# A mixture-of-experts layer: the combine stage replaced by weighing at PSUM and an adding indirect DMA

## What is computed

```python
gate_scores = softmax(x @ Wg + bg)                     # x: the layer-normed (2, 1024, 256)
topk_scores, topk_idx = top_k(gate_scores, 2)
topk_scores = topk_scores / (sum(topk_scores) + 1e-08)
for e in range(8):
    h = gelu(x @ W1[e] + b1[e])                        # W1[e]: 256x1024
    y = h @ W2[e] + b2[e]                              # W2[e]: 1024x256
    output = output + y * combine_w[..., e:e + 1]      # combine_w: topk_scores at the chosen experts
return x + output
```

## Time and profile before

| what | value |
|---|---|
| median of 3 runs | 1556.93 us (1554.15 to 1557.86) |
| profiled execution, span from first to last instruction | 1558.3 us |
| TensorE busy | 1257.4 us (81%) |
| TensorE weight loads | 752.1 us (48%) |
| VectorE busy | 840.2 us (54%) |
| ScalarE busy | 759.1 us (49%) |
| GpSimd busy | 279.8 us (18%) |
| mean granted TensorE clock | 0.886 |

### The profile page before, as it was taken

One profiled execution on the slowest core, in us unless ns is written; L12 is line 12 of the kernel. 1 busy time (PEld: TensorE's weight loads), 2 busy tenths in 40 slices (PEclk: granted clock), 3 DMA queues, 4 the chain that ended last, 5 costly groups with the idle time before them and its releaser, 6 DMA issues. The chain is left out here.

```text
span 1558.3 us, 26085 instructions
## 1 busy us (share of the span) xinstructions
PE 1257.4 (81%) x8850; PEld 752.1 (48%) x8851; DVE 840.2 (54%) x1883; ACT 759.1 (49%) x1473; POOL 279.8 (18%) x491
## 2 busy tenths in 40 slices
PE   4849999999999757974446999789875299999992
PEld 2313444444444245433125553554363299999991
DVE  4868777777777035336899545653255122322323
ACT  2815777777777713553654668235520033333330
POOL 1831222222222201102000000211023401111110
PEclk8958999999999967997558999989985599999996
DMA  5670312331230042000001000060026201111115
GB/s 198 210 225 15 70 36 69 74 72 33 73 70 16 13 122 90 1 1 21 1 0 32 1 2 1 27 230 1 5 61 196 86 28 37 37 34 37 37 33 170
DMA packets 63104, 96.09 MB, mean 62 GB/s; under 512 B 11057, under 2 KB 51923, under 8 KB 61459
## 3 DMA queue, kind: packets, MB, share of 16 engines
q1 hardware_dynamic: 56214, 78.14, 17.1%
q0 software_dynamic: 4672, 14.50, 2.8%
q10 hardware_dynamic: 2112, 2.10, 0.4%
HBM read 65.15 MB, written 29.17 MB: 61 GB/s over the span
## 5 line engine op out<-in xcount | busy, mean ns | idle before, releaser
L816 DVE CUSTOM_DVE_ANT_0 faded_scores_sb<-banks,inner_sb 128x1024 f32<-128x1024 f32 x256 | 304.5, 1223 | 102.2 <-PE banks L647 101.1
L915 ACT ACTIVATE xt_sb<-banks 128x512 f32<-128x512 f32 x344 | 179.0, 604 | 73.4 <-PE banks L654 73.4
L654 PE MATMUL banks<-q_stack_sb,k_stack_sb 99*128 99x128 bf16 (+3 forms) x960 | 181.0, 297 | 5.8 <-ACT xt_sb L915 2.6
L647 PE MATMUL banks<-k_stack_sb,q_stack_sb 96*128 96x512 bf16 (+3 forms) x704 | 163.9, 339 | 13.7 <-POOL ident_b_sb L744 9.4
L654 PEld LDWEIGHTS banks<-q_stack_sb,k_stack_sb 99*128 99x128 bf16 x960 | 71.7, 97 | 158.9 <-ACT xt_sb L915 66.6
L2074 PEld LDWEIGHTS banks<-slots_xt_sb,tile_w_sb 128*128 128x128 f32 x1248 | 146.6, 193 | 3.3 <-issue 1.4
L2074 PE MATMUL banks<-slots_xt_sb,tile_w_sb 128*128 128x128 f32 x1248 | 146.9, 276 | 1.0 <-DVE tile_b_sb L2172 1.0
L2086 PE MATMUL banks<-experts_w_sb,xt_sb 128*128 x624 | 141.2, 379 | 1.3 <-issue 1.3
L2086 PEld LDWEIGHTS banks<-experts_w_sb,xt_sb 128*128 128x128 f32 x624 | 115.5, 190 | 15.8 <-issue 1.7
L2120 ACT ACTIVATE slots_xt_sb<-banks 128x256 f32<-128x256 f32 x39 | 14.9, 383 | 213.9 <-PE banks L2060 213.9
L915 ACT ACTIVATE probs_sb<-banks 128x512 f32<-128x512 f32 x168 | 87.3, 605 | 34.2 <-PE banks L654 34.2
(11 more groups left out here) (303 smaller groups left out, 2081.8 us busy)
## 6 DMA issues: line engine op xcount, KB each, us to landing
experts_w_sb<-in_L_ffn_W SPq DMA_DIRECT2D x16, 1024.0 KB, 11.8
k_stack_sb<-k_parts SPq DMA_DIRECT2D x48, 256.0 KB, 4.9
q_stack_sb<-q_parts SPq DMA_DIRECT2D x96, 128.0 KB, 3.4
q_parts<-parts_sb SPq DMA_DIRECT2D x16, 384.0 KB, 2.7
k_parts<-parts_sb SPq DMA_DIRECT2D x16, 384.0 KB, 3.4
slots_x<-zeros_sb POOLq DMA_DIRECT2D x1, 5031.0 KB, 21.8
slots_x_sb<-slots_x SPq DMA_DIRECT2D x39, 129.0 KB, 2.0
xt_sb<-outputs_y SPq DMA_DIRECT2D x8, 512.0 KB, 6.5
```

The source lines that it names most:

```text
L647: last = pe.matmul(k.ps[:, 2 * (tile % 2) + half, lo - half * G:hi - half * G], stacks.q[0:ROWS, g % 3, version, h, j * P:(j + 1) * P], st ...
L654: return pe.matmul(k.ps[:, bank, at:at + hi - lo], stacks.k[0:ROWS + PARTS, g // 2 % 2, version, h, kt * P:(kt + 1) * P], stacks.q[0:ROWS ...
L816: dve.tensor_tensor_reduce(out=junk[:, tile % 2, :], in0=tile_scores(tile), in1=inner[:, window(tile)], scale=1.0, scalar=-3.0e38, op0=ALU ...
L915: act.activation(out, k.ps[:, bank_of((exp_done, u + 1)), :], ACT.Exp).then_inc(exp_done, 1)
```

## The change

A slot row gets three more values: both choices' experts (plus one) and both weights, next to the token's number, now stored minus `LATER` = 4096 so that an empty slot (zero) can be told apart. The weights are computed earlier in `route`, ahead of the scatters, and GpSimd waits for them. In `experts`, `take_rows` compares both choices with the tile's expert, multiplies by the weights, and adds the two to a share per row; the output row is the token, or one of 128 spare rows for an empty slot. The copy of y from PSUM multiplies by the share. The output has 128 spare rows; at the head of the block SyncE's queue writes `k.x` (x plus weighted b2) to it and zeros to the spare rows. Each scatter adds to the output in HBM, and waits on GpSimd for the scatter before it. The combine block and `outputs_y` are gone; the host slices the spare rows off.

```diff
-SLOT = D + 2
+SLOT = D + 5
+LATER = 2 * T
...
@@ route, GpSimd and VectorE @@
-            pool.wait_ge(numbered, 2)
+            pool.wait_ge(numbered, 4)
...
-            dve.tensor_scalar(xn[:, :, D + 1], at[:, :, 0], 1.0, None, ALU.add).then_inc(numbered, 1)
+            dve.tensor_scalar(xn[:, :, D + 1:D + 3], at[:, :, 0:2], 1.0, None, ALU.add).then_inc(numbered, 1)
...
+            step(dve.tensor_tensor(ssum[:, :], best[:, :, 0], best[:, :, 1], ALU.add))
+            step(dve.tensor_scalar(ssum[:, :], ssum[:, :], 1e-8, None, ALU.add))
+            step(dve.reciprocal(inv[:, :], ssum[:, :]))
+            for n in range(2):
+                dve.tensor_tensor(xn[:, :, D + 3 + n], best[:, :, n], inv[:, :], ALU.mult).then_inc(numbered, 1)
             dve.wait_ge(counted, 1)
...
-            step(dve.tensor_tensor(ssum[:, :], best[:, :, 0], best[:, :, 1], ALU.add))
-            step(dve.tensor_scalar(ssum[:, :], ssum[:, :], 1e-8, None, ALU.add))
-            step(dve.reciprocal(inv[:, :], ssum[:, :]))
+            dve.wait_ge(numbered, 4)
             for n in range(2):
-                step(dve.tensor_tensor(r.weight[:, n, :], best[:, :, n], inv[:, :], ALU.mult))
-                step(dve.tensor_tensor(hot[:, n, :, :], hot[:, n, :, :], wide(r.weight[:, n, :]), ALU.mult))
+                step(dve.tensor_tensor(hot[:, n, :, :], hot[:, n, :, :], wide(xn[:, :, D + 3 + n]), ALU.mult))
...
@@ experts, SyncE @@
-            sp.dma_start(idle[:, :], k.idle_in).then_inc(idle_in, 16)
+            sp.dma_start(spare[:, :], k.idle_in).then_inc(idle_in, 16)
+            sp.dma_start(out[0:T, :].rearrange("(t p) n -> p t n", p=P), k.x[:, :, :]).then_inc(out_in, 16)
+            sp.dma_start(out[T:T + P, :], k.zeros[:, 0:D]).then_inc(out_in, 16)
             bodies(sp, step)
...
@@ experts, GpSimd @@
                 pool.wait_ge(y_copied, n + 1)
+
+                if s > 0:
+                    pool.wait_ge(y_out[s - 1], (i + 1) * 16)
+                elif not (isinstance(i, int) and i == 0):
+                    pool.wait_ge(y_out[BODY - 1], i * 16)
                 pool.nop(nofuse=True)
-                pool.indirect_dma_start(out=scratch.y[:, :], out_offset=bass.IndirectOffsetOnAxis(ap=to[:, s:s + 1], axis=0),
-                                        in_=ys[:, s, :], in_offset=None).then_inc(y_out[s], 16)
+                pool.indirect_dma_start(out=out[:, :], out_offset=bass.IndirectOffsetOnAxis(ap=to[:, s:s + 1], axis=0),
+                                        in_=ys[:, s, :], in_offset=None, compute_op=ALU.add).then_inc(y_out[s], 16)
+            pool.wait_ge(out_in, 2 * 16)
             bodies(pool, step)
...
@@ experts, VectorE: take_rows, copy of y @@
-                dve.tensor_tensor(is_best[:, u:u + 1], xs[:, u, D + 1:SLOT], r.owned[:, tile], ALU.is_equal).then_inc(row_step, 1)
-                dve.wait_ge(row_step, 2 * (i * BODY + s) + 1)
-                dve.scalar_tensor_tensor(out=is_best[:, u:u + 1], in0=is_best[:, u:u + 1], scalar=float(T), in1=xs[:, u, D:D + 1],
-                                         op0=ALU.mult, op1=ALU.add).then_inc(row_step, 1)
-                dve.wait_ge(row_step, 2 * (i * BODY + s) + 2)
-                dve.tensor_tensor(to[:, u:u + 1], is_best[:, u:u + 1], idle[:, tile], ALU.max).then_inc(to_taken, 1)
+                dve.tensor_tensor(shares[:, u, :], xs[:, u, D + 1:D + 3], r.owned[:, tile].to_broadcast([P, 2]),
+                                  ALU.is_equal).then_inc(row_step, 1)
+                dve.wait_ge(row_step, 3 * (i * BODY + s) + 1)
+                dve.tensor_tensor(shares[:, u, :], shares[:, u, :], xs[:, u, D + 3:SLOT], ALU.mult).then_inc(row_step, 1)
+                dve.scalar_tensor_tensor(out=to[:, u:u + 1], in0=xs[:, u, D:D + 1], scalar=float(LATER), in1=spare[:, :],
+                                         op0=ALU.add, op1=ALU.min).then_inc(to_taken, 1)
+                dve.wait_ge(row_step, 3 * (i * BODY + s) + 2)
+                dve.tensor_tensor(share[:, u:u + 1], shares[:, u, 0:1], shares[:, u, 1:2], ALU.add).then_inc(row_step, 1)
...
-                dve.tensor_copy(ys[:, s, :], k.ps[:, 6, s * D:(s + 1) * D]).then_inc(y_copied, 1)
+                dve.wait_ge(row_step, 3 * n + 3)
+                dve.tensor_scalar(ys[:, s, :], k.ps[:, 6, s * D:(s + 1) * D], share[:, s:s + 1], None, ALU.mult).then_inc(y_copied, 1)
...
@@ program: combine (42 lines) and its call taken out @@
-            experts(k, r, scratch)
-            combine(k, r, scratch, out)
+            experts(k, r, scratch, out)
```

More of the change, by code:

```diff
@@ L1999, in _, with experts @@
                 dve.tensor_tensor(k.x[:, t, :], k.x[:, t, :], k.ps[:, 5 + t % 2, 0:D], ALU.add).then_inc(b2_added, 1)
-def experts(k, r, scratch):
+def experts(k, r, scratch, out):
     nc = k.nc
     k.next_block()
+    out_in = k.sem("out_in")
     x_in = [k.sem(f"x_in{u}") for u in range(2)]
@@ L2018, in experts @@
         xs = k.sb(c, "slots_x", [P, 2, SLOT])
-        is_best = k.sb(c, "is_best", [P, 2])
+        shares = k.sb(c, "shares", [P, 2, 2])
+        share = k.sb(c, "share", [P, 2])
         to = k.sb(c, "output_row", [P, 2], U32)
-        idle = k.sb(c, "idle_rows", [P, SLOT_TILES])
+        spare = k.sb(c, "spare_rows", [P, 1])
         xst = k.sb(c, "slots_xt", [P, 2, KD, P])
@@ L2190, in _ @@
                 dve.wait_ge(y_out[s], (NB + (s == 0)) * 16)
[L2193 to L2233, removed]
 INS = ["x", "L0_attn_W_down_kv", "L0_attn_W_up_k", "L0_attn_W_up_v", "L0_attn_Wq", "L0_attn_Wo",
@@ L2333, in program @@
             r.slot = k.sb(c, "slot", [P, 2, NT], U32)
-            r.weight = k.sb(c, "choice_weight", [P, 2, NT])
             r.owned = k.sb(c, "tile_owned", [P, SLOT_TILES])
@@ L2338, in program @@
             scratch.x = k.slots_x
-            scratch.y = nc.dram_tensor("outputs_y", (2 * T + SLOT_TILES * P, D), F32).ap()
             r.b1 = k.sb(c, "experts_b1", [P, E, FT])
@@ L2381, in layout @@
     a["c_iota"] = np.repeat(np.arange(IOTA, dtype=np.float32)[None, :], P, axis=0)
-    a["c_idle"] = np.ascontiguousarray(np.arange(SLOT_TILES * P, dtype=np.float32).reshape(SLOT_TILES, P).T)
-    a["c_numbers"] = np.ascontiguousarray((SLOT_TILES * P + np.arange(T, dtype=np.float32)).reshape(NT, P).T)
+    a["c_idle"] = T + np.arange(P, dtype=np.float32)[:, None]
+    a["c_numbers"] = np.ascontiguousarray((np.arange(T, dtype=np.float32) - LATER).reshape(NT, P).T)
     a["c_before"] = np.triu(np.ones((P, P), np.float32), 1)
@@ L2406 @@
          for n, a in arrays.items()}
-    out = nc.dram_tensor("out_0", (B, S, D), F32, kind="ExternalOutput").ap()
+    out = nc.dram_tensor("out_0", (T + P, D), F32, kind="ExternalOutput").ap()
     program(nc, d, out)
     got = run_bass_kernel_spmd(nc, [{f"in_{n}": a for n, a in arrays.items()}], core_ids=[0])
-    return got.results[0]["out_0"]
+    return np.asarray(got.results[0]["out_0"])[0:T].reshape(B, S, D)
```

## The result

The changed kernel takes 1567.31 us (median of 4 runs, 1566.79 to 1568.56) beside 1557.39 us for the kernel before: a ratio of 1.0069, 95% interval 1.0055 to 1.0083. It is about 10 us slower, where 6 us faster was forecast; it lies in the predicted range, and on the side of rival 1. The profiled execution's span is 1565.0 us.

A forecast was written before the change was run, and what follows sets the result against it. TensorE was taken to bound the experts' loop, the scatter's landing only just behind. End −24.7, preset +6.5 and loop +12.4 summed to −5.8 us: span 1552.5, or 1551 us on the median, range 1541 to 1582.

The forecast's parts named there:

- rival 1: Experts' loop, first row operation's wait: the adding scatter's landing becomes the bound; slower, up to 1589 us; chance 0.32.
- The accumulate, A: Each scatter in the experts' loop: adding to HBM costs 0.80 us extra, bounds 0 and 2.0.
- turning point of 1.1: Extra us per adding scatter at which the whole edit was forecast to gain 0.
- third list of descriptors: Part of the adding scatter's extra cost: 0.15 us taken, at most 0.28 for a list of 128.
- The read's later answer: Part of the adding scatter's extra cost: reading HBM answers later than SBUF, +0.15 us.
- The law of the loop: Experts' loop: time per tile is max(7.245, 7.09 + x/2, 6.41 + x), x being the added copy-to-choice time.
- middle branch: Time per tile 7.09 + x/2: from x = 0.31 to 1.36, half of each added us is lost.
- The small operations: Experts' loop: a fourth row operation 0.10 and two waits of 0.05 each; together 0.20 us, bounds 0.05 and 0.45.
- The preset: Start of the experts' stage: output stores ahead of the first slot fetch delay it by 6.5 us, bounds 0 and 9.7.
- The end: After the last scatter's issue: 3.6 us instead of 28.3, with 0.4 of closing, so −24.7 us.
- The gate weights: Moved ahead of the wait for the counts, where VectorE idles 1.30 us: about 0.97 us covered, nothing added.
- the clock: TensorE's clock stays at 1.00, the 2.4 GHz level, through the loop's gaps; no loss charged.

The follow-up runs named there:

- e1_plain: The changed kernel with the add taken out of its scatters, so each overwrites its output rows; 1540.64 us, ratio to the kernel before 0.9893.
- e7_rows64: The changed kernel with scatters of only the first 64 of 128 rows, at full width; single run 1553.48 us.
- e6_half: The changed kernel with scatters adding only the first 128 of 256 values of a row, to a tensor of its own; single run 1561.75 us.
- e9_before_add: The kernel before with scatters that add, to outputs_y filled with zeros by one more DMA; 1601.76 us, ratio 1.0286.
- e2_order: The changed kernel with the choice of weights ahead of the row operations in VectorE's order; 1541.47 us, ratio to the kernel before 0.9901.
- e3_preset: The changed kernel with the output preset moved into the routing stage as five stores; 1559.9 us, ratio to the kernel before 1.0006.
- e5_before_order: The kernel before with the choice of weights ahead of the row operations, nothing else; ratio 1.0006 over 12 runs.

## Why the prediction was wrong

The sign was wrong because of one term, the accumulate's, which was put at little more than half of what it took; the mechanism and its place were right.

**The accumulate, A.** The step that failed is "Second, the accumulate itself", A = 0.80. Measured: 3.8 us instead of 2.4, A = 1.4, above the turning point of 1.1. From copy to row operations it is 5.37 us in the mean, past the 4.9 that the prediction named as the sign of rival 1. DMA view of one plain scatter of the kernel before, from its issue to the row operations (40 slices of 0.065 us, busy share of the DMA engines), then of one adding scatter (slices of 0.099 us):

```profile
DMA  0000000000000000000000089798600000000000
...
DMA packets 48, 0.13 MB, mean 50 GB/s; under 512 B 16, under 2 KB 16, under 8 KB 48
```

```profile
DMA  0000000000000000000009951559999652000000
...
DMA packets 144, 0.13 MB, mean 33 GB/s; under 512 B 16, under 2 KB 144, under 8 KB 144
```

The plain one's packets run from 1.50 to 1.89 us after the issue, the adding one's from 2.07 to 3.36. So the start of the packets is 0.57 us later, where I took 0.15 for a third list of descriptors and thought 0.28 the most, from a zero fill that has no index per row; the issue on GpSimd grew by 0.59, which covers it. Little of that goes by the row: half the rows took 0.135 us off. What the rest is stays open. The packets last 1.29 us instead of 0.39, +0.90, where I took 0.50: there are 144, one per row, instead of 48 of up to 4 KB. The read's later answer, +0.15, doesn't show: the stretch after the last packet is 0.57 us, 0.69 before. The rule that an adding DMA moves at half the copy's rate, which the page gives for ring collectives (the Trainium skill, Collectives: The Full Stack, section "The bandwidth ceiling: the fold count and why AG ≠ RS ≠ AR") doesn't carry over: by it q0 would hold an engine 2 × 0.37 = 0.74 us a scatter, by an estimate; it held one 14.3% × 320 us / 38 = 1.20 us a scatter (its 5472 packets are those of 38 scatters), three times the plain 0.37:

```profile
q0 software_dynamic: 5472, 4.98, 14.3%
```

**The law of the loop** held. x is the mean of copy to row operations between 1300 and 1500 us, less 3.74 for the kernel before, and the period over 36 tiles:

| kernel | x, us | law | measured |
|---|---|---|---|
| e1_plain | 0.24 | 7.245 | 7.248 |
| e7_rows64 | 0.95 | 7.56 | 7.592 |
| e6_half | 1.10 | 7.64 | 7.681 |
| e9_before_add | 1.34 | 7.76 | 7.753 |
| changed kernel | 1.63 | 8.04 | 7.956 |
| e2_order | 2.44 | (choice not behind it) | 7.241 |

It came from one late landing in the trace of before, and is within 0.09 us at five values of x; in the changed kernel the stretch from row operations to copy had become 0.05 us shorter (2.61 for 2.66). Its middle branch is borne out by three kernels, the last (6.41 + x) by the changed kernel alone, at 0.08 us too much a tile.

**The small operations**, predicted 0.20, measured 0.24, with the shares elsewhere: the fourth row operation cost nothing (row operations to choice 2.71 instead of 2.73), the scaled copy takes 0.479 us instead of 0.424, and copy's end to issue went from 0.75 to 0.91 us, where I had 0.05; it is 0.91 in e1_plain and 0.74 in e9_before_add, so it comes with the added wait and not with the add.

**The preset** was right: +7.0 for +6.5, on the path because the fetch stands behind it (the first two fetches land 6.1 us after their issue, beside 2.0), and e3_preset takes 6.7 of it away. (The upper bound, 9.7, mixed KB of 1024 bytes with MB; it is 9.4.) **The end** was 2 us too cheap: 5.55 instead of 3.6. Of it 3.8 is the landing; the other 1.8 is the closing, from landing to the end of the span, after a GpSimd-issued DMA, which I had read from a store by ScalarE's queue (0.4). The plain scatters of e1_plain close the same way (4.48 for a landing of 2.4, so 2.1). The last wait also stands on another engine, VectorE here and ScalarE in the kernel before. What the 2 us consist of stays open. **The gate weights** cost nothing, as said; the clock did not fall in the gaps.

With A = 1.4 and x = 1.63 the prediction's own sum gives −25.5 + 1.4 + 6.5 + 28.6 = +11 us (the loop 36 × (8.04 − 7.245)), beside 9.9 measured. That they agree so well is partly luck: the loop comes out 4.3 us too dear (28.6 for 24.4) and the end, the preset and the stretches put at nothing 2.7 us too cheap together. Rival 1 had the case at 0.32, with the right mechanism. The prediction had the order on VectorE, but did not draw the conclusion from it: the landing only decides because the choice stands behind it in program order, and 26 us (1567.31 less 1541.47) lay in swapping two calls.

## What to carry to other kernels

A landing that is only just hidden is a price list: before an edit makes a DMA dearer, read the slack and what stands behind its wait in program order, and move the work that doesn't need the landing ahead of the wait. Small operations that are free by themselves cost nearly in full once another edit has used up the same slack, so price them together. A large store put on a queue ahead of a stage's first fetch is paid for at once; the stage before, beside an issue-bound scatter, had room for it.

## What the runs showed of the hardware that was not expected

- A scatter of 128 rows of 1 KB that adds takes 1.55 us of issue and lands after 3.8 us, beside 0.96 and 2.4 for one that overwrites; its packets are single rows (144 a scatter with the closing ones, beside 48).
- GpSimd's issue is held up by VectorE's copy of 128x2048 f32 from SBUF to SBUF: 1.55 us become 2.58 where they overlap (e2_order), and a plain scatter's 0.96 becomes 1.5 in the median, 2.0 at most (e5_before_order). The last three scatters of each kernel, which have no such copy beside them, keep 1.55 and 0.96, so the growth comes with the copy. Where the copy begins 0.05 to 0.55 us ahead of the issue, the growth is the overlap less about 0.1 us. This fits what the Trainium skill says (SBUF — State Buffer, section "SBUF: two separate sides"): the two engines share a pair of ports that one instruction holds to its end, and GpSimd can't write descriptors meanwhile. Where the issue begins first, some 0.13 us ahead of the copy (every other tile of e5_before_order), it grows by 0.51 us for 1.23 of overlap and the copy takes its usual 1.23, which that account doesn't give; so the ports are an explanation that no run here shows. In the kernels with the old order GpSimd's issue never met this copy, which is one more thing that the order decided.
- From the last landing to the end of the span pass 1.8 to 2.1 us after a scatter from GpSimd, and 0.4 after a store from ScalarE's queue. Which engine waits last differs too, and no run parts the two.
